# A windowed-attention stack on one core: the second MLP product from fp16 halves, two normalisations on ScalarE

## The reference, cut to what matters

```python
x = L0_attn_x                                   # (4, 2048, 256), fp32
x = x + layernorm(attention(layernorm(x)))      # first phase, full attention, softmax over the query axis
x = x + layernorm(ffn(layernorm(x)))            # second phase: two layers of

def _layer(x, ...):
    h = shift_token(x)                          # second half of the columns from the row before
    q, k, v = split(h @ wqkv)                   # 8 heads of 64
    q, k = rotary(l2norm(q) * qs, l2norm(k) * ksc)
    x = x + local_attention(q, k, v) @ wo       # windows of 128, own and previous window
    h = shift_token(x)
    h = (h - mean) / sqrt(var + 1e-5) * lg + lb
    a, g = split(h @ w1 + b1)                   # 682 columns each
    return x + (a * gelu(g)) @ w2 + b2
```

## Time and profile before

| | us |
|---|---|
| median of 3 runs (lowest, highest) | 3123.24 (3121.58, 3123.76) |
| the profiled execution | 3122.74 |
| its span, first to last instruction | 3120.9 |
| TensorE busy, share of the span | 2969.0, 95% |
| VectorE busy | 2654.2, 85% |
| ScalarE busy | 1876.3, 60% |
| POOL busy | 1742.8, 56% |
| mean granted TensorE clock | 0.979 of full speed |

### The profile page before, as it was taken

How to read it: one execution, slowest core, us unless ns; L and a number is a source line. 1 busy time by engine, 2 the same in 40 slices (tenths; PEclk the granted TensorE clock), 3 DMA queues, 4 the chain that set the end, 5 groups by cost and what they waited for, 6 DMA issues and landing times.

```text
span 3120.9 us, 79791 instructions
## 1 busy us (share of the span) xinstructions
PE 2969.0 (95%) x24952; PEld 2577.5 (83%) x24952; DVE 2654.2 (85%) x7701; ACT 1876.3 (60%) x4322; POOL 1742.8 (56%) x2070
## 2 busy tenths in 40 slices
PE   7999999945999999999999999999999999999997
PEld 4868686844888888888888888888888888888886
DVE  7889898656888888888888888898999999999995
ACT  6252525113666666667666766666666667666763
POOL 0313131125666666666666666676776677767763
PEclk9999999967999999999999999999999999999998
DMA  1212121151111111111111111122221211122121
GB/s 39 62 48 64 46 63 40 54 202 53 47 50 49 56 47 50 52 49 47 50 54 50 49 54 48 51 57 61 61 56 58 59 55 55 58 64 59 56 58 43
DMA packets 273326, 177.65 MB, mean 57 GB/s; under 512 B 95758, under 2 KB 271090, under 8 KB 272754
## 3 DMA queue, kind: packets, MB, share of 16 engines
q1 hardware_dynamic: 273138, 175.50, 19.2%
...
## 4 chain that ended last, share of the span: by engine, by line
PE 73%; POOL 1%; issue 1%; DVE 1%; ACT 0%; DMA 0%; POOLq 0%; SPq 0%; DVEq 0%; ACTq 0%
PE b_ps L869 17%; PE b_ps L944 14%; PE b_ps L955 10%; PE b_ps L897 8%; PE b_ps L885 7%; PE b_ps L923 6%; PE b_ps L910 6%; PE b_ps L854 2%; PE b_ps L847 2%; PE b_ps L836 1%; POOL b_sq L1190 0%; POOL b_rn L1223 0%; DVE b_probs L1138 0%; POOL b_t L1212 0%; DVE b_probs L1151 0%
## 5 line engine op out<-in xcount | busy, mean ns | idle before, releaser
L1002 ACT ACTIVATE b_probs<-b_probs,b_negmax 128x256 f32<-128x256 f32 x1024 | 505.9, 495 | 78.4 <-DVE b_negmax L1138 77.5
L869 PE MATMUL b_ps<-b_wqkv,b_hT_hi 128*128 128x512 f32 x1536 | 492.0, 402 | 1.0 <-DVE b_hT_lo L1026 1.0
L944 PE MATMUL b_ps<-b_h2T,b_w 128*128 128x256 f16 x4224 | 474.4, 274 | 6.4 <-DMA b_h2T<-b_xh_hl 6.4
L944 PEld LDWEIGHTS b_ps<-b_h2T,b_w 128*128 128x128 f16 x4224 | 414.5, 98 | 55.3 <-DMA b_h2T<-b_xh_hl 6.8
L1190 POOL TENSOR_TENSOR b_sq<-b_sq 128x512 f32<-128x512 f32 (+5 forms) x768 | 418.5, 545 | 60.6 <-ACT b_sq L983 20.3
L1223 POOL TENSOR_TENSOR b_rn<-b_ss_min,b_mhalf 128x16 f32<-128x16 f32 x128 | 377.5, 2949 | 109.2 <-DVE b_ss_min L1050 109.0
L1151 DVE TENSOR_SCALAR b_probs<-b_probs,b_rinv 128x256 f32<-128x256 f32 x1024 | 409.6, 442 | 18.2
L1200 POOL TENSOR_TENSOR b_rstd<-b_var,b_mhalf 128x1 f32<-128x1 f32 x128 | 72.0, 562 | 552.9 <-DVE b_var L1111 552.9
L452 PE MATMUL a_ps<-a_xn_hl,a_E 128*128 128x256 f16 x3072 | 344.5, 273 | 8.8 <-DVE a_E L318 8.8
L955 PE MATMUL b_ps<-b_w,b_hid 128*128 128x256 f32 x1536 | 342.2, 379 | 1.2 <-DVE b_hid L1174 1.2
L452 PEld LDWEIGHTS a_ps<-a_xn_hl,a_E 128*128 128x128 f16 x3072 | 299.4, 98 | 44.2 <-ACT a_e L397 9.6
...
## 6 DMA issues: line engine op xcount, KB each, us to landing
b_hx<-xs_dram SPq DMA_DIRECT2D x256, 64.0 KB, 1.9
b_rot<-rot_dram SPq DMA_DIRECT2D x128, 128.0 KB, 2.1
b_xr<-xs_dram SPq DMA_DIRECT2D x128, 128.0 KB, 2.0
xp_dram<-b_xp SPq DMA_DIRECT2D x128, 128.0 KB, 1.8
b_h<-xp_dram SPq DMA_DIRECT2D x256, 64.0 KB, 1.8
...
```

The costliest lines, as they stand in the source:

```text
L869: last = nc.tensor.matmul(ps[:, bank, :], hT[:, k, :], wqkv[:, ds(layer(s), 1), part, k, bank * INNER:(bank + 1) * INNER], start=(k == 0 a ...
L944: last = nc.tensor.matmul(ps[:, bank, half * 2 * P:(half + 1) * 2 * P], w1[:, ds(layer(2 * j), 1), wp, k, first:first + P], h2T[:, hp, k, ...
L1002: nc.scalar.activation(probs[:, h, :], probs[:, h, :], ACT.Exp, bias=negmax[:, h:h + 1], scale=-1.0, accum_out=rowsum[:, h:h + 1]).then_in ...
```

## The change

The second MLP product is made from fp16 high and low halves like the first: w2 is scaled by a power of two and split in the prologue, POOL splits `hid` into `hid_hl` block by block (blocks 0 to 3 at the end of its even slot, 4 and 5 early in its odd slot), and TensorE forms three partial products; the scale is undone in the layer output. The MLP input (`xh`, and its fp16 high half directly) and the layer-2 output (`fin`) are computed by ScalarE as `scale * x + shift`; VectorE gives the negated mean and POOL `shift = -mean * rstd`. On POOL one halving of the squares is left, and VectorE sums the other 32 columns (`sum_squares`); the power is split into k's eight columns, then kr, then q's eight. On VectorE the rotary products of the two half-heads become one instruction, two reciprocals replace four, `xp` stands ahead of normalise(0), and `sum_squares` stands between the output's statistics and oT_low. On ScalarE the v copy stands behind the probability copies. In the prologue w2 and b1 are loaded right after w1, and the scale of w1's first half also respects a bound on hid.

The core of the diff, cut; the prologue's scale arithmetic, declarations of tiles and semaphores are left out.

The prologue: SyncE (these loads stood behind b2's load), ScalarE, VectorE:

```diff
+                sp.wait_ge(cleared, 3)
+                for l in range(LAYERS):
+                    sp.dma_start(w2_f[:, l, 0:FULL, :], ...).then_inc(loaded_mlp, 16)
...
+                sp.dma_start(w2_f[0:REST, :, FULL, :], ...).then_inc(loaded_mlp, 16)
...
-                    nc.scalar.activation(w2[:, l], w2[:, l], ACT.Copy, scale=w1_unit[:, l:l + 1])
+                    nc.scalar.activation(w2[:, l, 0], w2_f[:, l], ACT.Copy, scale=w2_scale[:, l:l + 1]).then_inc(w2_hi, 1)
+                    nc.vector.tensor_reduce(top[:, 2, l:l + 1], w2_f[:, l].rearrange("p c d -> p (c d)"), AX.X, ALU.max, apply_absolute_value=True)
+                    nc.vector.scalar_tensor_tensor(w2[:, l, 1], w2_f[:, l], w2_scale[:, l:l + 1], w2[:, l, 0], ALU.mult, ALU.subtract)
```

TensorE, the second product:

```diff
-                        pe.wait_ge(hid_ready, HC * (j + 1))
+                        pe.wait_ge(hid_lo, HC * (j + 1))
...
-                                last = nc.tensor.matmul(ps[:, 3, n * D:(n + 1) * D], hid[:, c, n * P:(n + 1) * P], w2[:, ds(layer(2 * j), 1), c, :],
-                                                        start=(c == 0), stop=(c == HC - 1))
+                                for a, (hp, wp) in enumerate(PARTS):
+                                    last = nc.tensor.matmul(ps[:, 3, n * D:(n + 1) * D], hid_hl[:, hp, c, n * P:(n + 1) * P],
+                                                            w2[:, ds(layer(2 * j), 1), wp, c, :],
+                                                            start=(c == 0 and a == 0), stop=(c == HC - 1 and a == 2))
```

ScalarE:

```diff
-                        act.wait_ge(v_done, s + 1)
-                        wait(act, pv_done, s - 2)
-                        nc.scalar.copy(v[:, r, :], ps[:, 2, :]).then_inc(v_kept, 1)
+                    t = s - 3
+                    if in_range(t):
+                        act.wait_ge(shift2_ready, t + 1)
+                        wait(act, xh_lo, t)
+                        nc.scalar.activation(xh[:], h2[:, (r - 3) % 2, :], ACT.Identity, bias=shift2[:], scale=rstd2[:]).then_inc(xh_ready, 1)
+                        wait(act, h2T_loaded, 16 * t)
+                        nc.scalar.activation(xh_hl[:, 0, :], h2[:, (r - 3) % 2, :], ACT.Identity, bias=shift2[:], scale=rstd2[:]).then_inc(xh_hi, 1)
...
+                    if in_range(s):
+                        act.wait_ge(v_done, s + 1)
+                        wait(act, pv_done, s - 2)
+                        nc.scalar.copy(v[:, r, :], ps[:, 2, :]).then_inc(v_kept, 1)
...
+                        act.wait_ge(shiftf_ready, f + 1)
+                        wait(act, fin_stored, 16 * f)
+                        for n in range(2):
+                            nc.scalar.activation(fin[:, n, :], xpp[:, n, :], ACT.Identity, bias=shiftf[:, n:n + 1], scale=rstdf[:, n:n + 1]).then_inc(xf_ready, 1)
```

VectorE:

```diff
-                        nc.vector.tensor_tensor(t2_h[:, :, 0:half], x[:, :, half:DH], factor(2 * n + 1, 0, half), ALU.mult).then_inc(terms, 1)
-                        nc.vector.tensor_tensor(t2_h[:, :, half:DH], x[:, :, 0:half], factor(2 * n + 1, half, DH), ALU.mult).then_inc(terms, 1)
+                        nc.vector.tensor_tensor(by_half(t2[:, n, :]), by_half(ps[:, n, :])[:, :, ::-1, :],
+                                                factor(2 * n + 1).rearrange("p h (c d) -> p h c d", c=2), ALU.mult).then_inc(terms, 1)
...
+                def sum_squares(s):
+                    if in_range(s):
+                        dve.wait_ge(ss_halved, s + 1)
+                        wait(dve, ss_ready, s)
+                        nc.vector.tensor_reduce(ss[:], sq[:, :, 0:DH // 2], AX.X, ALU.add).then_inc(ss_summed, 1)
...
+                        nc.vector.tensor_scalar(negmean2[:], mv2[:, 0:1], -1.0, None, ALU.mult).then_inc(negmean2_ready, 1)
...
-                            nc.vector.tensor_tensor(xpp[:, n, :], ps[:, 3, n * D:(n + 1) * D], xb[:, (r - 6 + n) % 4, :], ALU.add).then_inc(xpp_ready, 1)
+                            nc.vector.scalar_tensor_tensor(xpp[:, n, :], ps[:, 3, n * D:(n + 1) * D], w2_unit[:, ds(layer(2 * j), 1)], xb[:, (r - 6 + n) % 4, :],
+                                                           ALU.mult, ALU.add).then_inc(xpp_ready, 1)
...
-                        nc.vector.tensor_scalar(xh[:], h2[:, (r - 3) % 2, :], mv2[:, 0:1], rstd2[:], ALU.subtract, ALU.mult).then_inc(xh_ready, 1)
-                        nc.vector.tensor_copy(xh_hl[:, 0, :], xh[:]).then_inc(xh_hi, 1)
                     rotate(s, r, 1, k_sq, k_terms, kr_ready)
                     output_stats(pairs - 3, r, layer)
+                    sum_squares(s)
                     oT_low(s - 2)
...
-                            dve.wait_ge(exp_done, HEADS * t + 2 * p + 2)
-                            nc.vector.reciprocal(rinv[:, 2 * p:2 * p + 2], rowsum[:, 2 * p:2 * p + 2]).then_inc(rinv_ready, 1)
+                            if p % 2 == 0:
+                                dve.wait_ge(exp_done, HEADS * t + 2 * p + 4)
+                                nc.vector.reciprocal(rinv[:, 2 * p:2 * p + 4], rowsum[:, 2 * p:2 * p + 4]).then_inc(rinv_ready, 1)
...
-                    normalise(0)
-                    normalise(1)
...
+                    normalise(0)
+                    normalise(1)
                     normalise(2)
...
-                    output_norm(pairs - 3, r, layer)
...
-                        wait(dve, w2_done, j)
+                        wait(dve, hid_lo, HC * j)
```

POOL:

```diff
+                def hid_halves(j, first, end):
+                    if in_range(2 * j):
+                        wait(pool, w2_done, j)
+                        for c in range(first, end):
+                            rows = slice(0, P if c < FULL else REST)
+                            wait_apart(pool, hid_ready, HC * j + c + 1, passed_pool)
+                            nc.gpsimd.tensor_copy(hid_hl[rows, 0, c, :], hid[rows, c, :]).then_inc(hid_hi, 1)
+                            pool.wait_ge(hid_hi, HC * j + c + 1)
+                            nc.gpsimd.tensor_tensor(hid_hl[rows, 1, c, :], hid[rows, c, :], hid_hl[rows, 0, c, :], ALU.subtract).then_inc(hid_lo, 1)
...
                         nc.gpsimd.tensor_tensor(rstd2[:], var2[:], mhalf[:, 0:1], ALU.pow).then_inc(rstd2_ready, 1)
-                    halve(s, 0, 2)
+                        pool.wait_ge(negmean2_ready, t + 1)
+                        pool.wait_ge(rstd2_ready, t + 1)
+                        nc.gpsimd.tensor_tensor(shift2[:], negmean2[:], rstd2[:], ALU.mult).then_inc(shift2_ready, 1)
+                    if r % 2 == 1:
+                        hid_halves(pairs - 2, HID_EARLY, HC)
+                        pool.wait_ge(k_sq, s + 1)
+                        nc.gpsimd.tensor_tensor(sq[:, :, 0:DH // 2], sq[:, :, 0:DH // 2], sq[:, :, DH // 2:DH], ALU.add).then_inc(ss_halved, 1)
...
-                        halve(s, 2, HALVINGS)
...
+                        nc.gpsimd.tensor_tensor(shiftf[:], negmeanf[:], rstdf[:], ALU.mult).then_inc(shiftf_ready, 1)
-                        nc.gpsimd.tensor_tensor(rn[:, r % 2, :], ss_min[:], mhalf[:], ALU.pow).then_inc(rn_ready, 1)
+                        nc.gpsimd.tensor_tensor(rn_k[:], ss_min[:, HEADS:2 * HEADS], mhalf[:, 0:HEADS], ALU.pow).then_inc(rnk_ready, 1)
...
+                        wait(pool, scores_kept, HEADS * (s - 1))
+                        nc.gpsimd.tensor_tensor(rn[:, r % 2, :], ss_min[:, 0:HEADS], mhalf[:, 0:HEADS], ALU.pow).then_inc(rn_ready, 1)
...
+                    if r % 2 == 0:
+                        hid_halves(pairs - 2, 0, HID_EARLY)
```

More of the change, by code:

```diff
@@ L42 @@
 SECOND_REST = P // 2
+A_COLUMNS = FULL * P + SECOND_REST
 assert 0 < REST <= P // 2
@@ L49 @@
 W1_TOP = 2.0 ** 13
+W2_TOP = 2.0 ** 13
+HID_TOP = 2.0 ** 14
+ROW_BOUND = 272.25
 NT = LAYERS * NW
@@ new lines, in _ @@
+                for l in range(LAYERS):
+                    dve.wait_ge(bias_added, l + 1)
+                    nc.vector.tensor_reduce(top[:, 1, l:l + 1], b1[:, l, :], AX.X, ALU.max, apply_absolute_value=True).then_inc(top_ready, 1)
+                    nc.vector.tensor_scalar(top_sq[:, l:l + 1], top_sq[:, l:l + 1], 2.0, None, ALU.mult).then_inc(top_ready, 1)
+                dve.wait_ge(top_shared, 2)
+                nc.vector.tensor_tensor(bias_sq[:], top_all[:, 1, :], top_all[:, 1, :], ALU.mult).then_inc(step, 1)
@@ L1005, in run @@
                         keep_hT(s + 1)
+                    j = pairs - 3
+                    f = j - NW // 2
+                    if r % 2 == 1 and in_range(2 * j) and layer(2 * j) == 1:
+                        act.wait_ge(shiftf_ready, f + 1)
+                        wait(act, fin_stored, 16 * f)
+                        for n in range(2):
+                            nc.scalar.activation(fin[:, n, :], xpp[:, n, :], ACT.Identity, bias=shiftf[:, n:n + 1], scale=rstdf[:, n:n + 1]).then_inc(xf_ready, 1)
                     j = pairs - 2
@@ L1181, in _ @@
             def _(pool):
-                def halve(s, first, end):
-                    if in_range(s):
```

(8 more changed lines are left out.)

207 lines of the change are left out of this document (118 added, 89 removed).

## The result

The changed kernel took 3212.75 us in the median of four runs (3210.10 to 3216.87), the kernel before 3123.50 beside it: a ratio of 1.0287 (95% interval 1.0269 to 1.0304). The forecast was 3042 with a range up to 3110: wrong, and on the other side. The profiled execution took 3216.87 us for a span of 3215.1.

The account below looks back on a forecast made before the run. TensorE, never waiting in steady state, was taken as the bound. 3122.74 - 83.4 (second product) + 6 (hT_lo) - 7 (ramp) + 2 (prologue) + 1 (tail) = 3041.3; the median is 0.5 higher, hence 3042 us, range 3024 to 3110.

Parts of the forecast that it names:

- A: POOL's odd-slot chain, by a cast dear as the subtraction or a late shift, eats 31 us: 3073; chance 0.17.
- B: POOL's cast so dear that its chain makes the kernel slower: 3159 to about 3300 us; chance 0.11.
- C: TensorE's second product: fp16 weight loads show, 149 ns a matmul, nothing gained: 3123 us; chance 0.04.
- The ramp's waits: TensorE's waits for kr at the second phase's ramp, 13.4 us, shrink with POOL's shorter chain: -7 us.
- The final normalisation (layer 2) goes the same way with slack: Moving layer 2's final normalisation to ScalarE, like the MLP input's, was taken to fit with slack; no cost charged.
- the 35.3 us needed: Forecast length of one pair of slots on TensorE, with TensorE still never idle; 36.58 us before.
- 3 us at hT_lo: By the port-lockout rule hT_lo could lose kr's full 1.04 us instead of 0.7; 3 us, inside the charge.
- collisions with POOL: In the prologue, a gain from fewer collisions was not excluded, but no row was said to price it.
- VectorE ... is not the bound, so this is worth nothing by itself.: VectorE's work falls by about 2 us a pair through smaller items; counted as worth nothing by itself.
- hT_lo, 0.1 us a pair (ends 0 and 0.7): Lateness of hT_lo ahead of TensorE's QKV product: 0.3 us spare, 6 us charged in all (ends 0 and 45).
- zero; up to 0.2 us a pair if the shift is late: ScalarE's two added affine operations ahead of the probsT copies delay TensorE by nothing, or 0.2 us a pair.
- Prologue, +2 (ends 0 and +9): Earlier w2 and b1 loads, two reductions and two low halves, partly beside transfers while VectorE idles for DMA: +2 us.

Follow-up runs that it names:

- run 5: Run 4 with the MLP input's statistics moved up on VectorE between qT_low and kT_low: 3063.64 us, 0.9823 of the kernel before.
- the pause: Changed kernel with POOL waiting for varf and negmeanf behind the halving in layer 2's odd slots: 3104.31 us, 0.9946 of the kernel before.
- run 11: Run 6 with POOL's prologue rotary products in four pieces per layer, ahead of its two reductions: 3060.53 us.
- run 9: Changed kernel with oT_low ahead of the output statistics and the reduction on VectorE: 3236.97 us, 1.0373 of the kernel before.
- run 4: Changed kernel with the pause, and hT_lo moved ahead of normalise(2) on VectorE: 3101.51 us.
- run 7: Run 6 with hT_lo put back behind normalise(2): 3086.35 us, 0.9884 of the kernel before.
- run 6: Run 5 with the w2 and b1 loads issued behind those of rotary factors and head scales: 3060.67 us, 0.9805 of the kernel before.

## Why the prediction was wrong, by its own steps

*Right.* The second product: 5.18 to 3.93 us a pair in layer 1, 1.25 for the 1.30 forecast. POOL's halves: 0.395 and 0.673 us for 0.43 and 0.675; powers of eight columns 1.65 and 1.82 for 1.68; the shift 0.19 for 0.3. The second product waited for the halves once, at the tail (3.0 us, for the 1 charged). So the dear cast of rivals A and B is false, and so is C; A's other way, a late shift, is a part of layer 1's loss (run 5). The result lies where B lay, and the sign named for A and B, TensorE idle before the output product, came too, but by another mechanism: oT_low stood behind varf and negmeanf. The ramp's waits gave 3.8 us of the 7 taken.

*The step that failed: "The final normalisation (layer 2) goes the same way with slack".* A pair of layer 2 became 3.0 us longer where it should have become 1.2 shorter; over 32 pairs the 3.0 alone are 96 us, about the whole loss (94 us of span), and the pause gives 108 back. Against the 35.3 us needed, layer 2's pairs are 4.3 us too long, 138 of the 171 us by which the forecast missed; layer 1's are 1.07 too long, 34. VectorE's varf was priced at nothing, as before. There it began while POOL had 0.2 us left of a short halving, and was done within the gap of 0.08 us behind it. But the change took five of the six dependent halvings from POOL's row and left four instructions back to back at that place, and added negmeanf behind varf. I asked of POOL's new order only when each result is ready, not what a POOL that no longer pauses does to VectorE's operations.

*The rule that was weighed at one place only.* I set a rule of the Trainium skill ("SBUF — State Buffer", the section on the port sides) against the 0.62 us of two scalings beside a power and let it count for 3 us at hT_lo. The section "Who interferes with whom" of that page of the Trainium skill says that a tensor_scalar in its two-port mode contends with GpSimd and that the later one is blocked for the whole instruction. The trace agrees with the blocking and goes further: in 14 slots varf was not served at the end of the instruction that held it, but after four of them (4.01 us, where 0.89 were left of the first), and in 15 negmeanf after three. In which mode varf runs, no run shows. The same section of the Trainium skill says that a tensor_reduce never contends; the trace agrees (677 ns in the slots, and 3.08 us in the prologue of run 11 as without POOL).

The trace of the kernel before already had the hold, in rows of its prologue that the prediction doesn't use:

```profile
668.95 1.82 DVE L652 TENSOR_SCALAR p_w_f<-p_w_f,p_lg 128x1408 f32<-128x1408 f32 x2 [20.19 <-PE b_ps L625]
...
678.26 7.68 DVE L652 TENSOR_SCALAR p_w_f<-p_w_f,p_lg 128x1408 f32<-128x1408 f32 x2 [4.38 <-PE b_ps L625]
...
675.51 8.82 POOL L613 TENSOR_TENSOR p_rot_all<-p_rot_all,p_head_scale 128x4096 f32<-128x4096 f32 x1 [22.88 <-DMA p_head_scale<-in_L_ffn_k_scale_dram]
```

Two gains of the same form took 1.82 us alone and 7.68 where they began beside POOL's rotary product, 1.6 us past its end. So the prediction's remark on collisions with POOL, that no row prices them, is wrong.

*"VectorE ... is not the bound, so this is worth nothing by itself."* Wrong for this kernel: in run 9, 1.18 us more of VectorE's work behind oT_low made a pair of layer 1 1.18 longer.

*hT_lo, 0.1 us a pair (ends 0 and 0.7).* The place was right and the size wrong: 0.45 (runs 4 and 7), inside the ends. kr falls on the scalings of normalise(0) and normalise(1), as forecast: the four take 2.00 us there, 0.76 more than twice 0.62, where 0.7 was taken.

*ScalarE, "zero; up to 0.2 us a pair if the shift is late".* It was late, and cost 0.45 in the even slot as soon as hT_lo didn't hide it, with some 0.2 a slot of longer products (run 5). The argument looked at the odd slot; in the even one VectorE's two layer outputs stand ahead of the statistics. Waits of equal length lay one behind the other, so that neither move alone was worth what both together were: hT_lo's gave 2.8 us (run 4), but 25.7 once the other was gone (run 7).

*Prologue, +2 (ends 0 and +9): 11.5.* "VectorE idles there for DMA" was wrong. With the loads back in order (run 6) 9.3 remain: two reductions over w2 of 1.74 us, 1.4 for a longer chain of scales, 3.5 for w2's low halves, and 0.9 for the rest ahead of the scales (small operations, a second reduction on POOL). The upper end, the sum over rows, was the better choice.
